# An operator of four attention and neighbour layers: loops as straight lists of calls, attention in halves of 512 columns, the second chunk layer in front of the full attention

## What is computed

```python
x = layer0(x, ctx)      # chunk attention: 8 heads of 16 channels, chunks of 64 positions
x = layer1(x, ctx)      # full attention: 32 heads, 8 key heads, with low-rank additions
x = layer2(x, ctx)      # chunk attention again, with other weights
x = layer3(ctx, x, k=30)

def layer0(x, ctx):     # layer2 is the same
    q, k, v = (proj(ctx, W, b) for W, b in three_parts(W_in, b_in))
    scores = einsum('bnqhd,bnkhd->bnhqk', q, k) * scale + mask
    out = softmax(scores) @ v
    out = (out @ W_out.T + b_out).T * masks + x
    return (out - mean(out)) * rsqrt(var(out) + EPS)

def layer1(h, ctx):     # q from h, k and v from ctx
    return h + lora(softmax(q @ k.T / sqrt(32)) @ v, Wo, Ao, Bo)

def layer3(p, x, k):    # p: the first coordinates of ctx
    idx = top_k(2 * p.T @ p - xx[:, None] - xx[None, :], k)[1]
    rel = p[idx] - p
    feat = spherical(rel)                    # radius, two angles
    att = softmax(three_small_layers_with_batch_norm(feat))
    return x + einsum('bnkc,bnk->bnc', x[idx], att)
```

## Time and profile before

| what | value |
|---|---|
| three timed runs | 8283.10, 8279.92, 8253.25 us; median 8279.92 |
| the profiled execution, its own time | 8271.05 us |
| its span, first to last instruction | 8269.3 us |
| mean granted TensorE clock | 0.859 of full speed |
| one pass of the loop over entries | see rows 2 |
| bytes moved by transfers | 482.41 MB, mean 58 GB/s |

### The profile page before, as it was taken

How to read it: one execution, slowest core, us unless ns; L and a number is a source line. 1 busy time by engine, 2 the same in 40 slices (tenths; PEclk the granted TensorE clock), 3 DMA queues, 4 the chain that set the end, 5 groups by cost and what they waited for, 6 DMA issues and landing times.

```text
span 8269.3 us, 204463 instructions
## 1 busy us (share of the span) xinstructions
PE 6884.4 (83%) x79422; PEld 4925.1 (60%) x79422; DVE 6179.9 (75%) x8508; ACT 4307.4 (52%) x9907; POOL 2685.8 (32%) x3399
## 2 busy tenths in 40 slices
PE   8888888888888888888888888888888759588888
PEld 5555555555555556555555555655555523488888
DVE  5777777777777777777777777777777747777777
ACT  3555555555555555555555555555555404566666
POOL 2333333333333333333333343333333310111111
PEclk9888888888888888888888888888888779899999
DMA  2111111111111111111111111111111130222222
GB/s 99 55 57 57 55 55 55 55 55 55 55 55 58 58 56 55 55 55 55 55 55 55 55 60 59 56 57 55 59 60 56 63 85 11 68 66 67 65 59 61
DMA packets 295563, 482.41 MB, mean 58 GB/s; under 512 B 103250, under 2 KB 216034, under 8 KB 293698
## 3 DMA queue, kind: packets, MB, share of 16 engines
q1 hardware_dynamic: 240205, 372.00, 15.1%
q10 hardware_dynamic: 54133, 94.55, 3.6%
HBM read 393.25 MB, written 73.25 MB: 56 GB/s over the span
## 4 chain that ended last, share of the span: by engine, by line
PE 54%; DVE 16%; ACT 15%; issue 10%; POOL 2%; DMA 1%; ACTq 1%; DVEq 0%; SPq 0%; POOLq 0%
ACT S L1047 6%; PE SCA L842 6%; PE PD L959 5%; PE SCA L811 4%; PE MISC L664 4%; PE SCA L946 3%; DVE m L1353 3%; ACT kexp L1090 3%; PE TP L834 3%; DVE pd L1359 3%; PE SCB L946 2%; PE PD L639 2%; PE SCA L682 2%; PE SCA L786 2%; PE TP L778 2%
## 5 line engine op out<-in xcount | busy, mean ns | idle before, releaser
L1353 DVE MAX8 m<-pd 128x8 f32<-128x1024 f32 x1024 | 1249.3, 1220 | 210.8 <-ACT pd L1016 99.0
L509 POOL TENSOR_TENSOR prod<-prod,hm 128x480 f32<-128x480 f32 x384 | 406.1, 1057 | 2928.8 <-ACT prod L1041 2762.2
L1357 DVE FIND_INDEX8 idx<-m,pd 128x8 uint32<-128x1024 f32 x1024 | 1248.7, 1219 | 9.5 <-issue 9.5
L1359 DVE MATCH_REPLACE8 pd<-m,pd 128x1024 f32<-128x1024 f32 x768 | 929.8, 1211 | 0.0
L639 PE MATMUL PD<-arena 128*128 128x512 f32 x1028 | 660.8, 730 | 149.7 <-ACT pd L1016 127.5
L664 PEld LDWEIGHTS MISC<-ptab,gat 128*128 128x128 bf16 x23400 | 673.8, 99 | 107.1 <-issue 77.7
L1600 DVE TENSOR_TENSOR gat<-maskT,con 120x2048 f32<-120x2048 f32 x256 | 592.1, 2352 | 171.2 <-PE SCA L946 162.3
L664 PE MATMUL MISC<-ptab,gat 128*128 128x24 bf16 x23400 | 667.5, 176 | 35.4 <-DVE gat L1309 20.6
L1047 ACT ACTIVATE S<-SCA,mx 128x64 f32<-128x64 f32 (+1 forms) x2560 | 572.0, 380 | 233.1 <-DVE mx L1365 233.1
L1365 DVE TENSOR_REDUCE mx<-SCA 128x16 f32<-128x1024 f32 (+1 forms) x192 | 235.2, 1225 | 506.9 <-PE SCA L767 456.1
L1047 ACT ACTIVATE S<-SCB,mx 128x64 f32<-128x64 f32 (+1 forms) x2560 | 570.9, 381 | 0.0
(11 more groups left out here) (270 smaller groups left out, 15192.6 us busy)
## 6 DMA issues: line engine op xcount, KB each, us to landing
gat<-low_scratch SPq DMA_DIRECT2D x396, 640.0 KB, 4.2
arena<-in_ctx ACTq DMA_DIRECT2D x33, 512.0 KB, 3.9
maskT<-in_mask ACTq DMA_DIRECT2D x32, 512.0 KB
arena<-in_x ACTq DMA_DIRECT2D x32, 512.0 KB, 6.3
x_scratch<-arena ACTq DMA_DIRECT2D x32, 512.0 KB, 4.8
x3T_scratch<-arena ACTq DMA_DIRECT2D x32, 512.0 KB, 3.7
arena<-x3T_scratch SPq DMA_DIRECT2D x32, 512.0 KB, 7.0
arena<-x_scratch SPq DMA_DIRECT2D x32, 512.0 KB, 9.3
```

The lines of the kernel that those rows point to most:

```text
L1353: step(V.max(m, buf[:, :]))
L1357: last = V.max_index(idx[:, t, 8 * r:8 * r + 8], m, buf[:, :])
L1359: step(V.match_replace(buf[:, :], m, buf[:, :], -3.0e38))
```

## The change

The three tables and the nested helpers go. Each engine's loop body is now one flat list of calls of small functions. The semaphore counts follow (24 halves for 12 groups, two normalisations `xl_done` for three, and so on).

- The unit of scores, maxima, exponentials, transposes, copies and value products is a half of 512 columns, one PSUM bank. `scores(s, h)`, `front(s, h)` and the others take the layer s (0 and 1 the chunk layers, 2 the full attention) and the half h of 8.
- `search(count)` issues the next `count` single operations of the search, wherever it stands. Each waits for the one before it by a semaphore of its own, as the rounds did.
- The second chunk layer comes before the full attention. Its masked output is kept in `X0` and added to `X1` (`residual(1)`); the full attention's projection is added last (`full_residual`), followed by the statistics and the scaling.
- The output projections of the chunk layers go through `TP`. The full attention's queries go in four pieces through `PD` (`query_pair`). Its keys are kept unexpanded in the end of `gat` (`k1_plain`) and expanded to `kexp` later.
- The result is transposed in two halves through `PD` in the next pass (`x3_half`), and stored then. `X0` is loaded later; the next context is loaded twice, once ahead into `hT` for its squares, once into `ctx`.
- SyncE loads the mask instead of ScalarE. GpSimd's `sides` of the pass stand after the split of indices, cut in four parts, and `turn` before `norm_parts`.

The core of the diff:

```diff
-        ROUNDS_AT = (0, 0, 1, 0) + (1,) * 8
-        DIST_AT = {2: (2, 0), 3: (2, 1), 4: (4, 1), 6: (5, 0), 7: (5, 1), 8: (7, 1)}
-        NORMS_AT = {9: 0, 10: 1, 11: 2}
# SyncE
             with sp.Fori(0, NB) as i:
+                sp.wait_ge(bias_ready, i + 1)
+                sp.wait_ge(res_done, i + 1)
+                for h in range(2):
+                    sp.dma_start(mb[96 + 3 * h:99 + 3 * h, :].rearrange("p (c k) -> p c k", k=CHUNK),
+                                 halves[0, :, h, :].partition_broadcast(3)).then_inc(mask_ld, 16)
+                sp.dma_start(maskT[:, :], mrow[0, :].partition_broadcast(P)).then_inc(mask_ld, 16)
# TensorE
+                def query_pair(pair):
+                    pe.wait_ge(hT_evac, i + 1)
+                    if pair:
+                        pe.wait_ge(pair_evac, i * 4 + pair)
+                    if pair != 2:
+                        pe.wait_ge(pd_evac, i * 16 + (9, 10, 0, 11)[pair])
+                    for c in (2 * pair, 2 * pair + 1):
+                        for kc in range(KC):
+                            last = mm(PD[:, c % 2 * P:(c % 2 + 1) * P], Wq[:, kc, c * P:(c + 1) * P],
+                                      hT[:, kc, :], start=(kc == 0), stop=(kc == KC - 1))
+                    last.then_inc(pair_ready, 1)
+                def turn_probs(s, h):
+                    pe.wait_ge(exp_done, i * 24 + 8 * s + h + 1)
+                    for j in range(4):
+                        o = h % 2 * 512 + j * P
+                        last = nc.tensor.transpose(SC[h // 2 % 2][:, o:o + P], S[h // 2 % 2][:, o:o + P], ident)
+                    last.then_inc(probsT_ready, 1)
+                keys(0)
+                chunk_values(0, 0)
+                queries(0)
+                chunk_values(0, 1)
+                distance(i, 1, 0)
+                scores(0, 0)
+                scores(0, 1)
+                turn_context()
+                split(i)
...
# ScalarE
-            def distance(b, t, h):
+            def distance(b, t, h, reused=True):
                 act.wait_ge(pd_ready, b * 16 + 2 * t + h + 1)
-                if t >= 2 and h == 0:
-                    act.wait_ge(topk_done, b * NT + t - 1)
+                if h == 0 and reused:
+                    act.wait_ge(topk_done, b * NT + t)
+                def evict(s, h):
+                    o = h % 2 * 512
+                    act.wait_ge(probsT_ready, i * 24 + 8 * s + h + 1)
+                    act.wait_ge(av_ready, i * 24 + 8 * s + h + 1)
+                    A(ET[:, o:o + 512], SC[h // 2 % 2][:, o:o + 512], ACT.Copy).then_inc(et_evac, 1)
# VectorE
-                def search_round():
+                def search(count):
+                    for _ in range(count):
+                        t, r = divmod(searched[0], 3 * ROUNDS - 1)
+                        r, part = divmod(r, 3)
+                        searched[0] += 1
...
+                def front(s, h):
+                    keys, g, half = (P if s == 2 else CHUNK), h // 2 % 2, h % 2
+                    rows = 512 // keys
+                    dve.wait_ge(scores_ready, i * 24 + 8 * s + h + 2)
+                    V.reduce_max(mx[g][:, half * rows:(half + 1) * rows],
+                                 SC[g][:, half * 512:(half + 1) * 512].rearrange("p (r k) -> p r k", k=keys), AX.X,
                                  negate=True).then_inc(front_done, 1)
+                search(1)
+                mask_bias()
+                search(3)
+                front(0, 0)
+                search(2)
+                front(0, 1)
...
+                onehot(i, 11)
+                search(2)
+                normalise(11)
+                search(14)
+                full_residual()
+                moments(X0)
+                search(2)
+                scaled(1, X0)
```

More of the change, by code:

```diff
@@ L519, in _ @@
             relative(0)
-            sides(0)
             steps = [0]
@@ L838, in _, with project_full @@
-                groups(1, scores1, values1)
-                distance(i, 6, 0)
-                for h in range(2):
+                def project_full(h):
+                    pe.wait_ge(ot_evac, i * 12 + 12)
+                    pe.wait_ge(et_evac, i * 24 + 26)
                     for c in range(KC):
@@ L856, in _ @@
+                norms(i + 1, 1)
+                outputs(11)
+                project_full(0)
+                norms(i + 1, 2)
+                project_full(1)
+                distance(i + 1, 0, 0)
+                distance(i + 1, 0, 1)
             pe.wait_ge(pd_evac, NB * 16 + 2)
+            for h in range(2):
+                x3_half(NB, h)
             split(NB)
             pe.wait_ge(split_evac, NB + 1)
+            pe.wait_ge(tab_done, NB * 2 + 2)
             for n in range(GROUPS):
@@ new lines, in _ @@
+                exponentials(2, 7)
+                distance(i, 6, 1)
+                evict(2, 4)
+                distance(i, 7, 0)
+                square()
+                pick(10)
+                output(8)
+                evict(2, 5)
+                distance(i, 7, 1)
+                output(9)
+                evict(2, 6)
+                evict(2, 7)
+                norms(i + 1, 0)
+                output(10)
+                angles(act, i)
+                norms(i + 1, 1)
+                output(11)
@@ new lines, in _ @@
+                load_context()
+                norms(i + 1, 2)
+                pick(11)
+                distance(i + 1, 0, 0)
+                distance(i + 1, 0, 1)
+                deviation(1)
+            act.wait_ge(xl_done, NB * 2 + 1)
+            act.dma_start(x3_dram[NB - 1, :, :], X0[:, :]).then_inc(x3_st, 16)
+            for h in range(2):
+                x3_half(NB, h)
+            act.wait_ge(tab_done, NB * 2 + 2)
+            act.dma_start(table_dram[NB - 1, :, :].rearrange("(t p) r -> p t r", p=P), tab).then_inc(table_st, 16)
```

1114 lines of the change are left out of this document (700 added, 414 removed).

## The result

The changed kernel takes 7528.2 us (median of 4 runs, 7513.0 to 7575.8) against 8266.6 for the kernel before (4 runs): a ratio of 0.916, 95% interval 0.912 to 0.920. Forecast were 7385 us, range 7120 to 7760. The time lies in the range, 143 us above the forecast. The profiled execution took 7537.6 us, its span 7535.0.

A forecast was written before the change was run, and what follows sets the result against it. It took VectorE's work plus its waits on other engines as the bound: 165.8 + 1.2 + 8.5 - 0.5 = 175.0 us a pass, down from 202.8. Over 32 passes, 890 us off and 4 on: 8271 to 7385 us, range 7120 to 7760.

The forecast's parts named there:

- its work stays 143 us at full clock: TensorE in one pass: unchanged counts of matmuls and transposes keep its work at 143 us at 2.4 GHz.
- TensorE 143 / 0.9 + 2.2 = 161: TensorE's time a pass: 143 us of work at clock 0.90 plus 2.2 for the jump, 92% of 175.
- Rival 2: TensorE becomes the bound, short waits on ScalarE keeping its clock at 0.84: 182.4 us a pass, 7622 us; chance 18%.
- The clock 0.88 to 0.92: Expected sign: TensorE's clock in the loop rises from 0.84 to between 0.88 and 0.92.
- VectorE's floor of 165.8: VectorE's time a pass at the old instructions without waits for other engines: 202.8 - 37.0 = 165.8 us.
- the period of 175.0: Length of one pass after the change: 165.8 + 1.2 + 8.5 - 0.5 = 175.0 us, from 202.8.
- 8.5 us of waits: VectorE's remaining waits a pass: 1.5 at the loop's head, 2 at its end, 5 at 35 other places.
- my signs of being wrong: Clock stays 0.84, a distance copy waits over 1 us for search in most passes, or one maximum over 3 each pass.
- Halves on VectorE, +1.2: VectorE's 12 row maxima of 1024 columns become 24 of 512: 0 to +1.8 us a pass, taken as +1.2.
- The order as the large term: Single search operations between short ones, independent matmuls from two layers, four banks in flight: the large term, leaving 8.5 us of waits.
- The loop's head: After the jump back, VectorE's first maximum waits for scores: 1 us, 2 if anything slips, taken as 1.5.
- Outside of the passes +4: Behind the loop, the last pass's transposes, stores and one side calculation stand alone: 0 to 15 us, taken as 4.

The follow-up runs named there:

- e2: The kernel before, with the first half's score matmuls all issued ahead of the second half's instead of in turns: 8502.8 us, ratio 1.033.
- e1: The changed kernel, with TensorE issuing the scores of a group's two halves together, their matmuls in turns, in all three layers: 7455.3 us, ratio 0.906.
- e5: The kernel before, with its neighbour search reading columns 0 to 511 of each distance row instead of all 1024: 7988.8 us, ratio 0.975.
- e10: The changed kernel, with VectorE's search in whole rounds again instead of operation by operation: 7545.5 us, ratio 0.919.

## Why the prediction was right, and where it failed

1. **"TensorE's matmuls and transposes stay the same in number ... so its work stays 143 us at full clock"**: the step that failed. The number did stay (55529 and 55588 records in the passes), the work became 158 us. I priced halves on VectorE and ScalarE and took TensorE's by count. 82 ns for a matmul of 256 columns, where a full one takes 226, meant partners beside it, and both rows were in the trace of the kernel before. e2 shows the cost by itself in the old kernel (+10 us), e1 its return (-11); some 4 of the 15 us are not located.
2. **TensorE 143 / 0.9 + 2.2 = 161, "tight but not the bound"**: with 158 in the place of 143 the same sum gives 158 / 0.9 + 2.2 = 177.8, above the 175.0 of VectorE. The one term would have turned the bound over. Rival 2 named the right engine and the wrong way to it: the clock did not stay at 0.84. Its 7622 us are 94 us off the measured time, the forecast's 7385 are 143.
3. **The clock 0.88 to 0.92**: right, 0.92. The busy time of 157 to 163 us: wrong by step 1, 171.5. That the clock follows the gaps in every row is a misreading: of the earlier trace rows one stretch is busy 85% at 0.77 and another 83% at 0.93.
4. **VectorE's floor of 165.8 and the period of 175.0**: only 4.0 us off, and that is luck. The forecast was a floor of 165.8 + 1.2 - 0.5 = 166.5 and 8.5 us of waits. Measured are a floor of 179.0 - 21.5 = 157.5 and 21.5 us of waits: 9 us too much and 13 too little. VectorE's waits for scores are 9.7 us, not 6, those for outputs 10.9, where I had them fall below 4.1. Its busy time is 150.9, not 155 to 158, and its idle time outside of the waits and the jump is 28.1 - 21.5 - 2.4 = 4.2 us a pass, where 47.5 - 37.0 - 2.1 = 8.4 stood before; I took 0.5 off. e5 shows that the floor was no bound of the kernel before, and the passes above that VectorE is not the bound of this one. Of my signs of being wrong none came: no distance copy waits for the search, and no maximum waits 3 us in each pass. The lists fail to meet at the outputs, where I had set no sign.
5. **Halves on VectorE, +1.2**: 24 maxima at 0.68 us against 12 at 1.22 make +1.6 in the rows. Right. VectorE's busy time fell all the same; the rows name 2.2 us of it (one-hot matrices 373.3 to 335.9 us in 31 passes, the scalings 87.8 to 56.2).
6. **The order as the large term**: right in kind, by the traces. TensorE's idle time fell by 25 us a pass, and that is the gain. The single search operations add nothing that e10 can tell. That the rest comes from two layers in flight and four banks is argued, not shown: no run takes either back.
7. **The loop's head**: the first maximum waits 1.70 us (1 to 2 forecast). ScalarE's 5.4 us no longer show as a gap ahead of the table load, since the load now waits for TensorE's keys (3.13 us in the pass shown). They were not all the jump before either: 1.5 of the 5.43 us are the issue of four transfers (0.41, 0.73 for two, and 0.36 us).
8. **Outside of the passes +4**: 8271.05 - 32 x 202.8 = 1781 before, 7537.6 - 32 x 179.0 = 1810 after, +29. The stretch behind the last mask bias was 1865.8 us and is 1884.7 here (+19, where at most 15 was forecast). It is 1841.7 in e1, which differs there only in the scores of the last pass, so a spread of this size is not the change's own.

The traced execution is 153 us above the forecast: 128 are the 4.0 us a pass, 25 lie outside.

## What to carry to other kernels

Before cutting a step of TensorE into halves, divide the busy time of its row by the count and compare it with a full-sized form of the same width: where it is far smaller (82 against 226 ns here), matmuls lie side by side, and a cut may take the partner away. An engine's work is not its instruction count. To see whether TensorE bounds, compare passes of one run that differ in clock: where the length moves one for one with its busy time it is the bound (it did not in the kernel before: 6.0 us of length for 13.6 of busy time). Taking work off it pays only if its in-order list has something ready for the place.

## What was not expected of the hardware

- Two sets of 8 matmuls on rows 0 to 63 and rows 64 to 127 take 1.03 us when issued in turns, and 2 x 1.01 one set after the other (plus the second bias). Two sets of the full attention's form, issued one after the other, do overlap: with halves (2, 1) and (2, 2) next to each other in the changed kernel,
```profile
2177.01 0.48 PE L823 MATMUL SCA<-kexp,reg 64*128 64x256 f32 x1
2177.05 0.46 PE L823 MATMUL SCB<-kexp,reg 64*128 64x256 f32 x1
2177.33 0.38 PE L823 MATMUL SCA<-kexp,reg 64*128 64x256 f32 x1
2177.34 0.38 PE L823 MATMUL SCB<-kexp,reg 64*128 64x256 f32 x1
```
they start in turns though all of SCA's stand ahead in the program. Why the chunk form does not was not tried; in it the second half's bias matmul (line 835) stands between the two sets.
- The granted clock falls to 0.50 for some 20 us in which TensorE is busy without a break (the rows above), behind 9 us in which it was busy 6.86. The 19 passes with a clock of 0.6 or less from 24 to 44 us behind their mask bias take 179.0 to 186.3 us, the other 12 take 172.1 to 179.5.
